# Matmuls on a constant matrix, written into TensorE's waits, in a perceiver block on one core

## The reference

```
x = x + xattn(layernorm(x), ctx)   # latent cross-attention: 16 heads, 128 context rows per sequence
x = x + attn(layernorm(x))         # one head of width 128: q, k, v = xn @ Wqkv + bqkv; softmax(q k / sqrt(128)) v @ Wo + bo
x = x + ffn(layernorm(x))          # xh = xn @ hadamard; 4-bit quantised rows of xh times ternary weights
return x

# xattn: C_q = Q @ Wq_d; C_kv = K @ Wkv_d
#        scores = (C_q @ W_qk per head) @ C_kv^T / sqrt(32); softmax; @ (C_kv @ Wv_u per head)
```

## Time and profile before

| | |
|---|---|
| Median of 3 runs | 355.42 us (355.22 to 356.23) |
| Span of the profiled execution, first to last instruction | 358.7 us |
| Mean granted clock of TensorE | 0.961 of full speed |
| Granted clock from 60 to 320 us | 1.00 |
| PE busy | 318.2 us (89%) |
| PEld busy | 221.9 us (62%) |
| DVE busy | 240.8 us (67%) |
| ACT busy | 207.5 us (58%) |
| POOL busy | 84.7 us (24%) |

### The profile page before, as it was taken

The page is one execution under the profiler, slowest core; times in us unless marked ns, Lnnn a source line. Parts: engine busy times, 40 slices in busy tenths (PEclk is TensorE's granted clock), DMA queues, the critical chain, the costliest instruction groups (busy, mean ns, idle before and its releaser), DMA issues.

```text
span 358.7 us, 8259 instructions
## 1 busy us (share of the span) xinstructions
PE 318.2 (89%) x3098; PEld 221.9 (62%) x3098; DVE 240.8 (67%) x515; ACT 207.5 (58%) x564; POOL 84.7 (24%) x126
## 2 busy tenths in 40 slices
PE   5879789999998999999999999899999999888682
PEld 3655666758585766666575858576766666565330
DVE  1399608777785858586877778585858586867312
ACT  1275566657565848485665857584849576561200
POOL 2001202222231323232222223132323232223101
PEclk9989969999999999999999999999999999999865
DMA  7882003030210303030403021030300010000000
GB/s 239 297 315 92 28 3 118 1 144 4 78 73 33 117 31 117 23 123 0 146 0 128 19 76 70 29 117 29 119 31 31 20 44 0 31 3 29 29 0 29
DMA packets 13336, 25.23 MB, mean 70 GB/s; under 512 B 3200, under 2 KB 3712, under 8 KB 13312
## 3 DMA queue, kind: packets, MB, share of 16 engines
q1 hardware_dynamic: 13312, 24.91, 19.8%
HBM read 20.71 MB, written 4.19 MB: 69 GB/s over the span
## 4 chain that ended last, share of the span: by engine, by line
DVE 49%; PE 26%; issue 14%; ACT 6%; POOL 3%; DMA 1%; DVEq 1%; POOLq 0%
DVE mx L401 11%; DVE sum_a L410 7%; PE ps L580 5%; PE ps L700 5%; PE ps L693 4%; PE ps L682 4%; ACT p L336 3%; DVE z L463 3%; DVE stat L427 3%; DVE x L424 3%; DVE xm L418 3%; DVE stat L444 3%; DVE stat L481 2%; POOL rstd L258 2%; DVE nmx L405 2%
## 5 line engine op out<-in xcount | busy, mean ns | idle before, releaser
L287 ACT ACTIVATE prob<-ps,nmx,qk_scale 128x128 f32<-128x128 f32 x256 | 96.5, 475 | 58.0 <-DVE nmx L405 58.0
L619 PE MATMUL ps<-had_s,x3t 128*128 128x512 f32 x128 | 62.0, 630 | 6.5 <-ACT x3t L281 6.5
L619 PEld LDWEIGHTS ps<-had_s,x3t 128*128 128x128 f32 x128 | 24.1, 198 | 38.2 <-issue 27.8
L401 DVE TENSOR_REDUCE mx<-ps 128x8 f32<-128x1024 f32 x32 | 39.0, 1220 | 10.9 <-PE ps L580 10.8
L410 DVE TENSOR_REDUCE sum_a<-prob 128x8 f32<-128x1024 f32 x32 | 37.5, 1210 | 2.3 <-ACT prob L287 2.3
L570 PE MATMUL ps<-ident,prob 128*128 128x128 f32 x256 | 33.7, 275 | 2.3 <-ACT prob L287 2.3
L281 ACT ACTIVATE prob_t<-ps 128x512 f32<-128x512 f32 x64 | 35.6, 634 | 0.0
L274 POOL TENSOR_TENSOR res<-prod,x 128x512 f32<-128x512 f32 x16 | 20.3, 1267 | 61.8 <-DVE prod L509 61.8
L636 PE MATMUL ps<-x2t,wqkv_s 128*128 128x128 f32 x256 | 32.8, 281 | 1.6 <-ACT x2t L281 1.2
L636 PEld LDWEIGHTS ps<-x2t,wqkv_s 128*128 128x128 f32 x256 | 29.8, 191 | 4.2 <-ACT x2t L281 3.1
L516 DVE SCALAR_TENSOR_TENSOR x<-ps,rsum,x2b 128x512 f32<-128x512 f32 x16 | 12.0, 750 | 28.5 <-PE ps L700 24.0
(11 more groups left out here) (107 smaller groups left out, 551.0 us busy)
## 6 DMA issues: line engine op xcount, KB each, us to landing
ct<-ctx_cols SPq DMA_DIRECT2D x16, 512.0 KB, 4.1
xt<-x_cols SPq DMA_DIRECT2D x16, 256.0 KB, 2.7
xr<-x_rows SPq DMA_DIRECT2D x16, 256.0 KB, 4.0
y<-res SPq DMA_DIRECT2D x16, 256.0 KB, 2.0
w_rows<-weight SPq DMA_DIRECT2D x1, 1024.0 KB, 8.6
had_s<-hadamard SPq DMA_DIRECT2D x1, 1024.0 KB, 7.9
wqkv_s<-wqkv SPq DMA_DIRECT2D x1, 768.0 KB, 9.5
wqk<-w_qk SPq DMA_DIRECT2D x2, 128.0 KB, 4.2
```

The costliest lines, as they stand in the source:

```text
L287: last = nc.scalar.activation(prob[:, h, :], ps[:, h // 4, (h % 4) * P:(h % 4) * P + P], ACT.Exp, bias=nmx[:, h:h + 1], scale=qk_scale[:])
L401: V.tensor_reduce(mx[:, h], ps[:, 2 * half:2 * half + 2, :].rearrange("p r (c k) -> p (r c) k", c=EC), AX.X, ALU.max).then_inc(done["mx"], 1)
L619: mm = pe.matmul(ps[:, B4, :], x3t[:, c, :], had_s[:, c, :], start=(c == 0), stop=(c == EC - 1))
```

## The change

A helper `keep_busy(count, bank)` on TensorE issues `count` float32 matmuls of `mean_w` with `mean_w`, 128x128, into the first 128 columns of a bank that holds nothing needed at that moment. No engine reads the result, and no semaphore is raised. The helper is called ahead of waits (or behind the group that precedes one) in rounds -1, 0 and 1 and in rounds 16 and 17: 33 source matmuls in the first part and 29 in the last, 62 in all. Nothing else is changed; the lists of the other four engines stay the same.

```diff
+            def keep_busy(count, bank):
+                for _ in range(count):
+                    pe.matmul(ps[:, bank, 0:P], mean_w[:], mean_w[:], start=True, stop=True)
+
             pe.wait_ge(consts_set, 3)
+            keep_busy(4, 0)
             pe.wait_ge(ld_w["wq"], 16)
...
             mm.then_inc(mean_made, 1)
+            keep_busy(1, 0)
...
                 if quant:
+                    if first and i == PAIRS + 1:
+                        keep_busy(3, 0)
                     after(pe, read["wo"], i - 2)
...
                 if first and i == 0:
+                    keep_busy(4, B1)
                     wide_bias()
...
                 if quant:
+                    if first and i >= PAIRS:
+                        keep_busy(2, 0)
                     after(pe, read["x3t"], i - 2)
...
                 if cross:
+                    if first and i == 0:
+                        keep_busy(2, B1)
                     transposed(0)
                     transposed(1)
                 if self_:
+                    if first and i == PAIRS:
+                        keep_busy(2, 0)
                     after(pe, read["x2t"], i - 1)
...
                     mm.then_inc(made["qkv"], 1)
+                    if first and i == 1:
+                        keep_busy(6, B2)
...
                 if quant:
+                    if first and i == PAIRS + 1:
+                        keep_busy(10, 0)
                     after(pe, done["qi"], i - 2)
...
                 if cross:
+                    if first and i == 0:
+                        keep_busy(8, B1)
                     transposed(2)
                     transposed(3)
                 if self_:
+                    if first and i == 1:
+                        keep_busy(5, B2)
+                    if first and i == PAIRS:
+                        keep_busy(2, 0)
                     after(pe, read["qkv"], i - 1)
...
                     mm.then_inc(made["s2"], 1)
+                    if first and i == PAIRS:
+                        keep_busy(5, 0)
                 if front:
+                    if first and i == -1:
+                        keep_busy(1, 0)
                     after(pe, read["lat"], i + 1)
...
                     mm.then_inc(made["ckv"], 1)
+                    if first and i == -1:
+                        keep_busy(2, 0)
...
                 if quant:
+                    if first and i == PAIRS + 1:
+                        keep_busy(2, 0)
                     after(pe, read["qit"], i - 2)
...
                 if self_:
+                    if first and i == PAIRS:
+                        keep_busy(1, 0)
                     after(pe, read["o2t"], i - 1)
```

## The result

| | before | changed |
|---|---|---|
| Median of 6 runs | 355.74 us (354.13 to 360.04) | 352.44 us (351.63 to 353.14) |
| Ratio to before | | 0.9899, 95% interval 0.9865 to 0.9932 |
| Span of the profiled execution | 358.7 us | 350.4 us |
| Mean granted clock in it | 0.961 | 0.994 |

The change makes the kernel faster by 1.0%, some 3.3 us; I had forecast 7.5 us and a time of 347.9, with a range that ended at 352.0. The direction was right, the size less than half.

A forecast was written before the change was run, and what follows sets the result against it. TensorE's half-speed stretches on the path at the start, in round 1 and at the end were taken as the loss: 5.0 + 1.6 + 1.2 - 0.3 = 7.5 us, from 355.42 to 347.9 us, range 346.2 to 352.0.

The forecast's parts named there:

- the one that carried the sum over: Whole kernel: 7.5 us off the 358.7 us span gives 351.2; keeping the 3.3 us distance to the median gives 347.9.
- The first rival: Timed executions hold less half-speed work than the profiled one, mainly at the end: 3.4 us gained, 352.0 us; chance 0.15.
- The evidence that I held against it: Against less half-speed work in the timed executions: the three timed runs lie within 1.0 us.
- start, to round 1's first scores: Start: clock rises before L580 (0.8 us) and partly before L669 (some 0.4), 1.2 us gained; at most 1.8.
- 0.3 off for the fillers: All filled waits: fillers that outlast their waits delay real matmuls, charged at 0.3 us altogether.
- round 1, from there to the start of its last product: Round 1: L663 to the end of L669 at full speed is 1.7 us shorter; 1.6 us taken.
- end, to the last quantised product: Rounds 16 and 17: L700 0.84, L593 0.46, L619 2.85 and L682 0.86 us at full speed; together 5.0 us.
- The price of an added matmul: In TensorE's waits: a filler is two matmul instructions, 0.24 us at full speed and 0.47 at half.
- The rival that a constant matrix does not count for the clock: Everywhere filled: clock falls as before and fillers only stand in the way, 358.4 us; chance 0.04.
- Its under 1%: Whole kernel: the skill's ramp penalty, at most 3.6 us here, a time of 351.8 or more; not used as cap.

The follow-up runs named there:

- first profile: The kernel before, unchanged, as profiled for the prediction: span 358.7 us, mean granted clock 0.961; its six timed runs have a median of 355.74 us.
- second profile: The kernel before, run again with no edit: profiled span 353.4 us, clock 0.977; 357.07 us median of 12, ratio 1.0005.

## Why the prediction was wrong

The step that failed is the one that carried the sum over: "The span is 3.3 us above the median of the runs; I carry the difference over". Time is span plus 1.8 us in every execution. A span 3.3 us above the median of the times therefore said that this execution was about 5 us longer than the median one, and that the half-speed work in it was not that of the median one. Even without the constant, a span is part of its execution's time, and 358.7 is more than all three times. The first rival had this mechanism and nearly the right time (352.0 for a measured 352.44), with a chance of 0.15. That it came so near is in part luck: in the second pair of profiles its 1.2 for the start measured 0.3 and its 1.6 for round 1 measured 2.0. The evidence that I held against it, three runs within 1.0 us of each other, was no evidence about the profiled execution, which was not one of the three.

By terms, in us, against the first profile and against the second one of before:

| term | predicted | first profile | second profile |
|---|---|---|---|
| start, to round 1's first scores | 1.2, and 0.3 off for the fillers | 30.23 - 29.21 = 1.0 | 29.54 - 29.21 = 0.3 |
| round 1, from there to the start of its last product | 1.6 | 22.34 - 20.29 = 2.0 | 22.29 - 20.29 = 2.0 |
| rounds 2 to 15, to L588 of round 16 | 0 | 270.39 - 270.32 = 0.1 | 270.21 - 270.32 = -0.1 |
| end, to the last quantised product | 5.0 | 31.09 - 25.98 = 5.1 | 26.73 - 25.98 = 0.75 |
| sum | 7.5 | 8.2 | 3.0 |

- The end: right group by group, wrong as a forecast of the median. Against the second profile the term is 0.75, all of it L682's (1.80 - 1.04). That the 5.1 of the first profile belongs to the quarter of the executions with a clock of 0.966 or less is likely; only one of them was profiled.
- Round 1: mechanism right, size a fifth too small (1.6 for 2.0). I had measured L663 to L669 (1.7) and left out L655 before and the groups up to L700 behind, which were at half speed too.
- The start: in the changed kernel's profile the clock was up by L692 at 8.5, sooner than I assumed, though in other runs with the same start it rose as late as L586, and the transfer of the weights was the bound, at 16.41 where I had 16.1. But round 0, to which I gave no cost, gave back 0.5 us in this profile: L540 waited 3.13 us for `wo_s`, the clock fell behind it, and the fillers then ran at half speed ahead of needed transposes. Over the profiles with round -1's matmuls of 128 columns, round 1's first scores lie anywhere from 28.28 to 29.90 us, so what the start gains in a typical execution isn't shown by one pair.
- The price of an added matmul: 0.24 us predicted, 0.22 to 0.24 measured, and what outlasts a wait is paid.
- The rival that a constant matrix does not count for the clock is refuted: round 1 stays at 1.00 with it. With 8 columns in place of 128, the same constant did not keep rounds 0 and 1 up.
- The rule of the Trainium skill that the number of slow matmuls differs from run to run (section "What's actually happening" of "TensorE: Matmul & The Clock Gate") agrees with the traces here: the end's half-speed work was 5.1 us in one profile of before and 0.75 in the other. It should have had far more weight than 0.15. Its under 1% is for the ramp; in the trace the added matmuls gave back 1.0 or 0.3 us at the start, under 1% too. Most of the 8.2 us (2.3%) and the 3.0 us (0.8%) between the pairs of profiles was later falls, so the figure was never a cap on the sum.

## What to carry to other kernels

Before a sum is made from one profile, compare its span with the timed runs: if their distance isn't the constant one that other profiles show, the profile is of an unusual execution, and its half-speed stretches are that execution's. Matmuls put into TensorE's waits paid here where they fitted the wait, were 128 columns wide, and stood near places where the clock falls in most executions: eight at the start gave most of the median's gain, and with twelve near the end none of twelve executions was among the long ones. The ratio doesn't show the second kind of gain: look at the mean and the longest too, and compare them only with executions of before from the same turns.

## What the runs showed of the hardware

- Executions of one kernel, one core at a time, have mean granted clocks between 0.955 and 0.990 and times between 353.9 and 362.3 us, with nothing changed; those at 0.966 and less took 4.5 us more in the mean than the group from 0.970 to 0.977. The share at 358 us and above ran from 0 of 12 on one occasion to 28 of 71 on others.
- TensorE with an instruction in hand for 9.9 us without a gap stayed at half speed (0.50) while weight loads and 8-column matmuls made up part of it; with 128 columns at the same places it was at half speed for 3.5 us.
- The granted clock reads 1.00 at the start of every profile here, where durations are those of half speed (L663 at 8.5 us took 2.08 us, against 1.16 later).
- In a profile with eight added matmuls at the start and none in round 1, the clock stayed up in round 1, 30 us later; in one with the same eight and round 0's fourteen it fell there. No run here explains this.
